# Composing the second weight factor inside the attention slots, with one output bank

## The reference

```python
# 1 differential attention, 16 heads, two softmax maps per head of width 8
attn = softmax(mask(Q1 @ K1.T)) - lam * softmax(mask(Q2 @ K2.T))
O = rmsnorm(attn @ V);  x = x + O @ Wo
# 2 feed-forward, with weights that are composed from 32 low-rank primitives (32 = top-k of 32)
W1 = einsum('k,kir,kro->io', softmax(fc1_logits), fc1_A, fc1_B)   # 128 x 512
W2 = einsum('k,kir,kro->io', softmax(fc2_logits), fc2_A, fc2_B)   # 512 x 128
x = x + gelu(x @ W1) @ W2
# 3 causal linear attention, then the feed-forward a second time
```

## Time and profile before

| what | us |
|---|---|
| median of 3 runs | 428.15 (424.87 to 428.99) |
| the profiled execution | 431.64, of which 429.9 from the first to the last instruction |
| PE / DVE / ACT / POOL busy | 367.9 / 308.9 / 237.0 / 198.4 |

### The profile page before, as it was taken

One profiled execution on the slowest core, in us unless ns is written; L12 is line 12 of the kernel. 1 busy time (PEld: TensorE's weight loads), 2 busy tenths in 40 slices (PEclk: granted clock), 3 DMA queues, 4 the chain that ended last, 5 costly groups with the idle time before them and its releaser, 6 DMA issues.

```text
span 429.9 us, 9985 instructions
## 1 busy us (share of the span) xinstructions
PE 367.9 (86%) x3316; PEld 236.1 (55%) x3316; DVE 308.9 (72%) x989; ACT 237.0 (55%) x582; POOL 198.4 (46%) x319
## 2 busy tenths in 40 slices
PE   0599697097999898998999898899989989999995
PEld 0466486085555554655554555444866656664774
DVE  5596855079899888897979796864665789998110
ACT  3332521003688778787878686762856244353822
POOL 6223422001558667575758584840016557883000
PEclk9999979569899999999999999969999999999999
DMA  7879998990133313132223200000000000000001
GB/s 207 269 244 309 219 244 243 214 200 10 46 96 88 79 46 83 41 86 57 77 77 76 77 4 5 2 3 2 0 2 0 2 0 0 2 1 0 26 25 50
DMA packets 48930, 34.50 MB, mean 80 GB/s; under 512 B 20080, under 2 KB 43760, under 8 KB 48880
## 3 DMA queue, kind: packets, MB, share of 16 engines
q1 hardware_dynamic: 48880, 33.86, 32.0%
HBM read 25.20 MB, written 8.39 MB: 78 GB/s over the span
## 4 chain that ended last, share of the span: by engine, by line
PE 46%; DVE 19%; SPq 10%; issue 10%; ACT 5%; DMA 4%; POOL 4%; DVEq 0%; POOLq 0%; ACTq 0%
PE ps L1373 6%; PE ps L1164 6%; PE ps L1364 5%; PE ps L1088 5%; SPq L402 3%; PE ps L1096 3%; DVE arena L1506 3%; SPq L430 2%; PE ps L1083 2%; DVE arena L1519 2%; PE ps L1577 2%; PE ps L1168 2%; DVE arena L1025 2%; ACT arena L832 2%; PE ps L1240 2%
## 5 line engine op out<-in xcount | busy, mean ns | idle before, releaser
L784 POOL TENSOR_SCALAR_AFFINE_SELECT arena<-arena 128x256 f32<-128x256 f32 (+1 forms) x192 | 90.1, 484 | 94.5 <-ACT arena L832 90.5
L832 ACT ACTIVATE arena<-ps 128x512 f32<-128x512 f32 x192 | 109.3, 603 | 27.9 <-PE ps L1122 27.7
L1025 DVE TENSOR_REDUCE arena<-ps 128x4 f32<-128x1024 f32 x64 | 78.3, 1223 | 13.0 <-PE ps L1096 10.0
L1018 DVE CUSTOM_DVE_ANT_0 ps<-ps,future 128x128 f32<-128x128 f32 x256 | 66.2, 320 | 10.5 <-PE ps L1083 10.5
L1447 POOL TENSOR_TENSOR arena<-arena 128x1024 f32<-128x1024 f32 x16 | 34.1, 2133 | 40.3 <-DVE arena L1532 40.3
L1122 PE MATMUL ps<-stacks 50*128 50x256 bf16 x256 | 50.6, 278 | 0.3 <-ACT arena L832 0.2
L1088 PE MATMUL ps<-stacks 48*128 48x256 bf16 x256 | 40.8, 276 | 2.2 <-DVE arena L1025 1.9
L1164 PE MATMUL ps<-arena,values 128*17 128x256 f32 x512 | 40.9, 392 | 0.0
L475 POOL TENSOR_TENSOR qk_parts_sb<-qk_rest,qk_parts_sb 128x512 bf16<-128x512 f32 x16 | 19.1, 1211 | 42.1 <-DVE qk_parts_sb L559 42.1
L1018 DVE DVE_READ_ACCUMULATOR2_ANT arena<- 128x1 f32 x256 | 36.1, 141 | 0.0
L1577 PE MATMUL ps<-arena,upto 128*128 128x384 f32 x96 | 35.9, 486 | 0.0
(11 more groups left out here) (140 smaller groups left out, 715.8 us busy)
## 6 DMA issues: line engine op xcount, KB each, us to landing
stacks<-qk_parts SPq DMA_DIRECT2D x96, 128.0 KB, 3.3
qk_parts<-qk_parts_sb SPq DMA_DIRECT2D x16, 384.0 KB, 4.9
arena<-in_L_ffn_fc_B_dram SPq DMA_DIRECT2D x4, 1024.0 KB, 7.9
arena<-in_L_ffn_fc_A_dram SPq DMA_DIRECT2D x16, 256.0 KB, 5.8
xs<-in_L_attn_a_X_dram SPq DMA_DIRECT2D x4, 256.0 KB, 4.0
qk_parts<-qk_parts_sb SPq DMA_DIRECT2D x8, 128.0 KB, 5.3
arena<-in_L_ffn_fc_B_dram SPq DMA_DIRECT2D x4, 256.0 KB, 5.0
stacks<-arena SPq DMA_DIRECT2D x64, 4.0 KB
```

Of the source, the lines that this page charges most:

```text
L784: nc.gpsimd.affine_select(out=diag, in_=diag, compare_op=ALU.is_ge, fill=0.0, base=0, pattern=[[0, 2 if s < 2 else UMAPS], [1, P]], channe ...
L832: nc.scalar.activation(probs[:, r, s, :], ps[:, bank, :], ACT.Exp, scale=SCALE).then_inc(exp_done, 1)
L1018: last = nc.vector.tensor_tensor_reduce(out=block, in0=block, in1=future[:], scale=1.0, scalar=LOWEST, op0=ALU.add, op1=ALU.max, accum_out ...
L1025: nc.vector.tensor_reduce(out=rowmax[:, gs, 1, UMAPS * uu:UMAPS * (uu + 1)], in_=ps[:, S_BANK + 1:S_BANK + 3, :].rearrange("p b (m k) -> p ...
```

## The change

The second factor's work leaves the projection and the first six attention slots. Its chunks are spread over attention slots 1 to 62. DVE turns chunks 0 and 1 behind slots 1 and 2, and each later chunk c behind slot 4c-2. PE does all four products of chunk 0 in slot 2, and from slot 3 to 62 one product a slot, between the output projection and `both(it, j, 1)`. They add up in a bank of their own (`W_BANK`, 6), so that only one output bank (5) is left, and weighted values wait for the copy of the unit before. b2 and quarter 0 of a2 are loaded behind sequence 7; the other quarters go two DMAs at a time between the stores of shifts. The scaling of b2 goes behind slot 1 on ACT, W2's copy behind slot 62. a2 and b2 get places of their own in the arena.

```diff
-        FACTORS = (((0, 1), ()), ((2,), (0,)), ((3,), (1,)), ((), (2,)), ((), (3,)), ((4, 5), ()),
-                   ((6, 7, 8), (4, 5, 6)), ((9, 10, 11), (7, 8, 9)),
-                   ((12, 13), (10, 11)), ((14, 15), (12, 13)), ((16,), (14, 15)), ((17, 18), (16,)),
-                   ((19,), (17, 18)), ((), (19,)))
+        FACTORS = (((0, 1), ()), ((2,), (0,)), ((3,), (1,)), ((), (2,)), ((), (3,)), ((), ()), ((), ()), ((), ()))
+        def turned_chunk(slot):
+            if slot in (1, 2):
+                return slot - 1
+            c = (slot + 2) // 4
+            return c if (slot + 2) % 4 == 0 and 2 <= c < KR else None
+        def second_products(slot):
+            if slot == 2:
+                return [(0, j) for j in range(FCH)]
+            c = (slot + 1) // 4
+            return [(c, (slot + 1) % 4)] if 1 <= c < KR else []
+        SECOND_END = 4 * KR - 2
...
-                if b == 2:
-                    load_fc2_b()
-                if 3 <= b < 5:
-                    load_fc2_a(b - 3)
...
-            load_fc2_a(2)
-            load_fc2_a(3)
+            load_fc2_b(sp)
+            load_fc2_a(sp, 0)
...
-                if b == 4:
-                    scale_second_factor(act)
...
             store_shift(0, 0)
+            load_fc2_a(sp, 1, (0, 2))
...
                     load_stack(sp, g + 4, k)
+                    if g < 5:
+                        load_fc2_a(sp, (g + 3) // 2, (0, 2) if g % 2 == 1 else (1, 3))
...
-        S_BANK, T_BANK, O_BANK, M_BANK = 0, 3, 5, 7
+        S_BANK, T_BANK, O_BANK, W_BANK, M_BANK = 0, 3, 5, 6, 7
...
             def head(slot):
-                if slot == HEAD_SLOTS - 1:
+                if slot == 1:
+                    scale_second_factor(act)
+                if slot == SECOND_END:
                     act.wait_ge(acc_done, FGROUPS)
-                    nc.scalar.copy(w2[:]..., ps[:, ACC_BANK, :]).then_inc(w12_done, 1)
+                    nc.scalar.copy(w2[:]..., ps[:, W_BANK, :]).then_inc(w12_done, 1)
...
             def head(slot):
-                if slot < HEAD_SLOTS:
-                    scale_factors(dve, SEQS + slot)
-                if slot == HEAD_SLOTS:
-                    dve.wait_ge(fT_done, FGROUPS)
-                    nc.vector.memset(ps[:, O_BANK:O_BANK + 2, 0:SEQ], 0.0).then_inc(cleared, 1)
+                if slot == 0:
+                    dve.wait_ge(fT_done, 4)
+                    nc.vector.memset(ps[:, O_BANK, 0:SEQ], 0.0).then_inc(cleared, 1)
+                c = turned_chunk(slot)
+                if c is not None:
+                    turn_factor(dve, c)
...
-                    if past(n - 1):
-                        pe.wait_ge(ot_copied, n - 1)
+                    if past(n):
+                        pe.wait_ge(ot_copied, n)
...
+            def second_factor(slot):
+                for c, j in second_products(slot):
+                    if c == 0 and j == 0:
+                        pe.wait_ge(b2_scaled, KR // 2)
+                    pe.wait_ge(fT_done, 4 + c + 1)
+                    product = nc.tensor.matmul(ps[:, W_BANK, j * P:(j + 1) * P], a2T[:, c % 4, j * P:(j + 1) * P],
+                                               b2[:, c, :], start=(c == 0 and j == 0),
+                                               stop=(c == KR - 1), skip_group_check=True)
+                    if j == FCH - 1:
+                        product.then_inc(acc_done, 1)
...
                 output_projection(it, j)
+                second_factor(SLOTS * it + j)
                 both(it, j, 1)
                 both(it, j, 2)
...
             def head(slot):
-                if slot < HEAD_SLOTS:
-                    factors_tensor(pe, SEQS + slot)
+                pass
```

More of the change, by code:

```diff
@@ L185, in hybrid_kernel @@
         late_end = at
+        a2, at = carve(late_end, (KR // 2, F // BLK, R))
+        b2, at = carve(at, (KR, D))
         def part_of(u, side, part):
@@ L317, in scale_factors, with turn_factor @@
             for i in FACTORS[slot][0]:
[L318 to L330, removed]
+                dve.wait_ge(fT_ps, i + 1)
+                nc.vector.tensor_tensor(
+                    a1T[:, 4 * i:4 * i + 4, :],
+                    ps[:, FT_BANK + i % 2, :].rearrange("p (c d) -> p c d", c=4),
+                    mix_col[:, 4 * i:4 * i + 4].unsqueeze(2).to_broadcast([P, 4, P]),
+                    op=ALU.mult).then_inc(fT_done, 1)
+        def turn_factor(dve, n):
             dve.wait_ge(fc2_a_in[n // 4], 16 * P // BLK)
-            dve.wait_ge(acc_done, max(4, i - 3))
+            dve.wait_ge(acc_done, max(4, n + 1))
             nc.vector.transpose(a2T[:, n % 4, :].rearrange("p (j b) -> p j b", b=BLK),
@@ L355, in factor_products @@
             def factor_products(i):
[L356 to L360, removed]
+                pe.wait_ge(fc1_b_in[i], 16)
                 pe.wait_ge(fT_done, i + 1)
                 for j in range(4):
[L363 to L372, removed]
+                    c = 4 * i + j
+                    last = nc.tensor.matmul(ps[:, ACC_BANK, :], a1T[:, c, :], b1[:, c, :],
+                                            start=(c == 0), stop=(c == KR - 1))
                 last.then_inc(acc_done, 1)
@@ L378, in factors_tensor, with load_fc2_a, load_fc2_b @@
                     factor_products(behind[n])
-                if n < len(ahead) and ahead[n] < 4:
+                if n < len(ahead):
                     factor_transposes(ahead[n])
+        def load_fc2_a(sp, quarter, blocks=(0, 2, 1, 3)):
+            for i in blocks:
+                k = PRIMS * BLK // P * i + 2 * quarter
+                sp.dma_start(a2[BLK * i:BLK * (i + 1), 2 * quarter:2 * quarter + 2]
+                             .rearrange("p c j r -> p (c j) r"),
+                             fc2_A[k:k + 2].rearrange("k (j p) r -> p (k j) r", p=BLK))\
+                  .then_inc(fc2_a_in[quarter], 16)
+        def load_fc2_b(sp):
+            for i in (0, 2, 1, 3):
+                k = PRIMS * BLK // P
+                sp.dma_start(b2[BLK * i:BLK * (i + 1)],
+                             fc2_B[k * i:k * (i + 1)].rearrange("k (e p) f -> p (k e) f", p=BLK))\
+                  .then_inc(fc2_b_in, 16)
         def project_sync(sp):
@@ L396, in load_fc1_b @@
                   .then_inc(fc1_b_in[quarter], 16)
[L398 to L408, removed]
-                    k = PRIMS * BLK // P
-                    sp.dma_start(b2[BLK * i:BLK * (i + 1)],
-                                 fc2_B[k * i:k * (i + 1)].rearrange("k (e p) f -> p (k e) f", p=BLK))\
-                      .then_inc(fc2_b_in, 16)
             load_fc1_b(0)
@@ L707, in turns @@
                     emit(it, j)
-                    if it == 0 and j <= HEAD_SLOTS:
-                        head(j)
+                    head(SLOTS * it + j)
             for j in range(L_STAT - UPS + 1):
@@ L849, in emit @@
                         act.wait_ge(ott_done, n - 1)
-                    nc.scalar.copy(ot_sb[:, r, :], ps[:, O_BANK + r, 0:SEQ]).then_inc(ot_copied, 1)
+                    nc.scalar.copy(ot_sb[:, r, :], ps[:, O_BANK, 0:SEQ]).then_inc(ot_copied, 1)
                 n = unit(it, j, L_OT)
@@ L902, in head @@
             def head(slot):
-                if slot == HEAD_SLOTS - 1:
+                if slot == 1:
+                    scale_second_factor(act)
+                if slot == SECOND_END:
                     act.wait_ge(acc_done, FGROUPS)
-                    nc.scalar.copy(w2[:].rearrange("p a b -> p (a b)"), ps[:, ACC_BANK, :]).then_inc(w12_done, 1)
+                    nc.scalar.copy(w2[:].rearrange("p a b -> p (a b)"), ps[:, W_BANK, :]).then_inc(w12_done, 1)
             turns(act, emit, amid, head)
@@ L1163, in weigh_values @@
                     if t == 0:
-                        nc.tensor.matmul(ps[32 * m:32 * m + DV + 1, O_BANK + r, 0:SEQ], values[:, tile, head, :],
+                        nc.tensor.matmul(ps[32 * m:32 * m + DV + 1, O_BANK, 0:SEQ], values[:, tile, head, :],
                                          probs[:, p, m // 2, m % 2 * SEQ:m % 2 * SEQ + SEQ],
@@ L1167, in weigh_values @@
                     else:
-                        last = nc.tensor.matmul(ps[32 * m:32 * m + DV + 1, O_BANK + r, P:SEQ],
+                        last = nc.tensor.matmul(ps[32 * m:32 * m + DV + 1, O_BANK, P:SEQ],
                                                 values[:, tile, head, :], probs[:, p, 2, m * P:(m + 1) * P],
```

12 lines of the change are left out of this document (5 added, 7 removed).

## The result

The changed kernel takes **459.71 us** (median of 4 runs, 459.64 to 460.03), the kernel before 427.08 in the runs beside it: a ratio of 1.075 (95% interval 1.0705 to 1.0795). It is slower, as forecast, but by 32.6 where the forecast had 12.4. The profiled execution took 460.03, of which 458.2 from the first to the last instruction. In the new file the lines are: values L1159 and L1163, product L1174, scores of bank 1 L1083, exponentials L824, copy of the weighted values L842, turn L340, maxima L1012.

A forecast was written before the change was run, and what follows sets the result against it. It took PE and DVE, nearly full in attention, to bound the kernel. 428.15 + 18.5 (loss, slots 8 to 63) - 6.0 (gain up to slot 8) = 440.6, stated as 440.5 us; own range 432 to 448, with rivals 430 to 448.

The forecast's parts named there:

- the price of the product: One product on PE between weighted values and bank 1's scores, taken as 0.13 us from a row of them.
- the loop: Attention with one bank: values, product, bank 1's scores, two exponentials, copy, next values; 2.83 us a plain slot, 26.05 for eight.
- the upper bound of 0.25: Highest price given for a product in the loop, if a lone one does not overlap its weight load.
- The turn in slot 3: The product waits there for DVE's turn of a chunk; bounds 0 and 0.65 us, taken as 0.15.
- Slot 4: Slot with transposed maxima (+0.36) and ACT's roots holding the second exponential 0.86 behind bank 1; predicted 3.62 us.
- I take 18.1 unchanged: Slots 2 to 7 keep 18.1 us: products leaving might save 6.1, half clock might add about 2.5.
- its 6.1: Slots 2 to 7: time saved if all 48 products at 0.13 us were on the path and left.
- the whole gain of 6.0: Up to slot 8: earlier fc2 loads start slot 2 at 84.2 instead of 90.25; gain between 2 and 13 us.
- 1 falls: Rival, attention: PE does not wait for the copy, only the head's 6.0 remains, faster at 422 us; chance 0.10.
- 2 falls: Rival: the head gives 13 us and the loop is at its cheap end, no change, 428 to 432; chance 0.12.
- rival 3: Attention loop: one slot in eight falls to half clock, 1.2 us each, 7 times, 449 us; chance 0.08.
- Rival 4: SP's queue in attention: a2 loads hold the stores of shifts, 1.5 us in five groups, 448; chance 0.06.

The follow-up runs named there:

- run 5: The changed kernel with each product made twice, so the second factor comes out doubled; 476.82 us, ratio 1.1175.
- run 1: The kernel before with one change alone, a single output bank, so weighted values wait for the copy of the unit before; 439.76 us, ratio 1.0263.
- Run 2: The changed kernel without 60 of its 64 products (only chunk 0 multiplied), turns, loads and waits kept; 440.27 us, ratio 1.0283.
- Run 9: The changed kernel with 44 overwritten products more in slot 2, keeping TensorE busy in the hole; 459.8 us.
- run 4: The changed kernel with the product moved to the end of PE's slot, behind masks and transposes; 436.92 us, ratio 1.0179.
- run 10: Against the changed kernel with product last and copy ahead of the second exponential: loads and products moved so nothing in slots 1 and 2 waits for fc2; 429.96 us.
- run 11: Run 10 with quarter 0 of a2 and b2 loaded behind the first store and stack 3, chunks turned from slot 10 on; 423.87 us, ratio 0.9925.
- run 12: Run 11 with at most four fc2 transfers between two stores of shifts, scaling from slot 11, turns from slot 17; 417.10 us, ratio 0.9732.

## Why the prediction was wrong, and where it was right

**The step that failed** is the price of the product: "24 of the present ones take 3.04, 0.13 each". The row counts records, and 24 records are 12 products, so that the same row gives 0.25. In the loop it measured 0.42 in plain slots, over even the upper bound of 0.25, which was meant for a lone product and is what the row gives for one among others. The cross-check was at hand: 64 products stand as 128 records in the page of before too. With 0.42 in place of 0.13 the predicted plain slot is 2.83 + 0.29 = 3.12, which is what the table has.

The Trainium skill (FP8 and Floating Point Precision, TensorE Precision Notes) has true fp32 going through the array in four passes. An estimate by it, 128 columns four times at 2.4 GHz, is 0.213 us; the 0.22 of the second product in run 5 agrees.

**The rest of the loop was right.** In slot 29: values to product 0.78 (predicted 0.78 to bank 1), bank 1 to exponential 0.43 (0.43), exponential to end of copy 1.35 (1.35), hand-over 0.15 (0.14). The bank alone was predicted at 26.05 - 1.04 - 0.15 = 24.86 in eight slots and measured 24.78 in run 1. The turn in slot 3 cost 0.24 (0.15). Slot 4 came out at 3.43 (3.62), because the roots cover the product. In all, slots 8 to 63 took 188.4 in place of 176.1: **12.3 of the miss**. Run 2 puts 17.2 on the 55 products there (188.4 against 171.2), where 0.13 each makes 7.2: 10.0 of the 12.3.

**The second step that failed** is "I take 18.1 unchanged" for slots 2 to 7. They took 22.7 (85.85 to 108.54) at the half clock, which the same paragraph had named and priced at 2.5. Run 9 puts 2.6 on the clock in two of these slots, and run 4 takes 5.2 off them at the same half clock: the products that are left, which the paragraph weighs only as a gain, stand in front of bank 1's scores. What each of the two is worth without the other was not measured. (Its "48 products" are 48 records of 24 products, so its 6.1 is right all the same.) SP's queue was as worked out: past sequence 7's stores at 70.4 (predicted 70.1). Slot 1's turn came at 85.21 (predicted 83.6, bounds 80 to 85). Together slot 8 came 6.2 later than predicted (102.3): the whole gain of 6.0 went. By the Trainium skill (TensorE: Matmul & The Clock Gate, Part 1) the low level is the default and sustained activity lifts it. The trace agrees: PE is busy 2.11 of 20.00 in the hole, and the clock rises behind 4.00 busy of 4.00 in 108 to 112.

The sum: 12.3 + 6.2 = 18.5, less 2.7 by which the stretch behind slot 63 is shorter (161.3 for 164.0), is 15.8. The 2.7 goes with the clock: in the first 40 us behind slot 63 it is granted at 1.00 in after and at 0.90 and 0.93 in the two halves in before; what sets it there is open. Another 3.2 is the base: before's profiled execution lay 3.5 above its median, after's 0.3. That makes 19.0 of the 19.2 between 440.5 and 459.7.

**The rivals.** The copy is waited for in 49 of the 55 slots behind slot 8 (1 falls), and the head gave nothing (2 falls). The clock of rival 3 did fall, but in the head and not in the loop, which stands at 1.00 from 113 to 300. Rival 4's hold-up doesn't show in after, where SP's pairs fit; with more transfers ahead of a store it did, in run 10 (4.80) and, beside ACT's wait for b2, in run 11 (7.55).

## What to carry to other kernels

Before pricing an instruction by a row's count, divide the count by the program's own number of such instructions: fp32 matmuls leave two records here. Before giving up a second buffer, write down the loop that closes, and look for an order in which nothing dear stands inside it: the same products and the same single bank cost 1.075 in one order and 1.002 in another. After a hole in front of a stage, read the clock at which the stage starts, here 0.50. And look at what stands ahead of a small store on its queue: behind eight large loads (run 11) it let PE go only 7.5 after its issue, behind four just issued (run 10) 6.7; in run 12, where the store comes 5.9 after the first of four, no such wait was left.

## What the runs showed of the hardware that was not expected

- One fp32 product of 128 x 128 took 0.22 us behind another, 0.23 behind the transposed maxima with their 16 columns of weights, and 0.42 behind the weighted values; its price depends on its neighbour.
- The granted clock stayed at 0.50 for the 22 us from 86 to 108, though PE was busy 17.90 of them. In run 9 it was at 1.00 in the six microseconds from 85, after 44 products, and fell again behind 3.65 busy of 6.00.
- In run 11 a store of 4 KB transfers issued at 93.21 let PE go on only at 100.72, with eight transfers of 256 KB issued in the 8 us ahead of it; the last of these let ACT go on at 100.17.
